# A fused adaLN + block-sparse FFN kernel: x loads one slot closer to their use, and the logits of the early batches turned and ranked behind the layer

## What is computed

```
z1 = einsum('bfi,bir->bfr', x, v) / 512
z  = einsum('bfr,bor->bfo', z1, u) / 16
y  = gelu(einsum('bfi,oi->bfo', x, W) + fc_bias + z + b)      # the layer
prob = softmax(y @ w_router + b_router); idx = top_k(prob, 4)  # the router
h = relu(einsum('nd,ebd->neb', y, w1b) + b1b)
out = x + einsum('neb,ebd,ne->nd', h, w2b, mask(idx)) + b2
```

## Time and profile before

| | us |
|---|---|
| three runs | 1649.1, 1648.52, 1642.79 (median 1648.52) |
| the profiled execution, its own time | 1648.12 |
| span of the profile | 1646.3 |
| PE busy | 951.5 (58%) |
| DVE busy | 837.2 (51%) |
| ACT / POOL busy | 583.9 / 576.1 (35% each) |
| granted TensorE clock, mean | 0.785 |
| DMA queues of SP / POOL, share of 16 engines | 38.5% / 21.2% |

### The profile page before, as it was taken

How to read it: one execution, slowest core, us unless ns; L and a number is a source line. 1 busy time by engine, 2 the same in 40 slices (tenths; PEclk the granted TensorE clock), 3 DMA queues, 4 the chain that set the end, 5 groups by cost and what they waited for, 6 DMA issues and landing times.

```text
span 1646.3 us, 17908 instructions
## 1 busy us (share of the span) xinstructions
PE 951.5 (58%) x4924; PEld 765.4 (46%) x4924; DVE 837.2 (51%) x1966; ACT 583.9 (35%) x1063; POOL 576.1 (35%) x589
## 2 busy tenths in 40 slices
PE   8755656466556465565565479866888898400000
PEld 7543545355445354454354357654777777300000
DVE  4432333333334242343343346563786786698777
ACT  6332333233233242333333245552665566200000
POOL 0554431332333323243423426556444344400000
PEclk9977787787777777787777789987999999755555
DMA  5765443534543534434434557657668765799999
GB/s 188 257 236 188 147 162 121 177 126 147 170 143 143 170 107 166 162 135 159 167 120 153 176 185 249 237 210 257 223 223 271 263 209 204 273 419 427 425 430 395
DMA packets 103234, 354.82 MB, mean 216 GB/s; under 512 B 29961, under 2 KB 29961, under 8 KB 92384
## 3 DMA queue, kind: packets, MB, share of 16 engines
q1 hardware_dynamic: 59104, 217.21, 38.5%
q0 software_dynamic: 43936, 136.37, 21.2%
q10 hardware_dynamic: 96, 0.10, 0.0%
HBM read 200.47 MB, written 169.65 MB: 225 GB/s over the span
## 4 chain that ended last, share of the span: by engine, by line
PE 39%; DMA 26%; issue 11%; DVE 8%; another core or an unknown queue 6%; SPq 5%; ACT 4%; POOL 1%; ACTq 1%; DVEq 0%; POOLq 0%
DMA tabi<-table 15%; PE hid L1310 9%; PE trn L1294 8%; PE lay L1204 8%; DMA w2l<-yt 8%; PE yps L1341 5%; PE hid L1315 3%; DVE xs L813 2%; PE hid L1190 1%; DVE stx L1026 1%; PE trn L1224 1%; ACT xs L585 1%; DMA outT<-ys 1%; PE lay L1341 1%
## 5 line engine op out<-in xcount | busy, mean ns | idle before, releaser
L547 POOL DMA_INDIRECT yt<-ys,ids x238 | 256.0, 1076 | 450.0 <-ACT ys L690 332.0
L1294 PE MATMUL trn<-idf,gr 128*128 128x128 f32 x720 | 127.8, 334 | 354.8 <-DMA tabi<-table 327.5
L521 POOL DMA_INDIRECT xg<-grow,ix x224 | 219.5, 980 | 231.5 <-DVE ix L909 167.5
L1294 PEld LDWEIGHTS trn<-idf,gr 128*128 128x128 f32 x720 | 105.5, 173 | 373.7 <-DMA tabi<-table 335.6
L1204 PE MATMUL lay<-w2l,xs 128*128 128x512 f32 x768 | 199.6, 411 | 0.0
L1204 PEld LDWEIGHTS lay<-w2l,xs 128*128 128x128 f32 x768 | 147.9, 198 | 31.0
L633 ACT ACTIVATE gsb<-trn 128x512 fp32r<-128x512 f32 x144 | 81.0, 598 | 190.8 <-PE trn L1294 187.5
L844 DVE TENSOR_TENSOR above<-gr,tabi 128x12 f32<-128x12 int32 x45 | 7.6, 169 | 263.5 <-DMA tabi<-table 263.5
L633 ACT ACTIVATE xs<-trn 128x512 fp32r<-128x512 f32 x88 | 50.4, 597 | 211.5 <-PE trn L1294 160.5
L835 DVE TENSOR_TENSOR gsb<-trn,gsb 128x512 fp32r<-128x512 f32 x144 | 94.5, 686 | 55.4 <-ACT gsb L633 48.9
L663 ACT ACTIVATE hv<-hid,b1c 128x512 f32<-128x512 f32 (+1 forms) x94 | 52.7, 584 | 191.2 <-PE hid L1315 159.8
(11 more groups left out here) (220 smaller groups left out, 2026.0 us busy)
## 6 DMA issues: line engine op xcount, KB each, us to landing
gr<-xg SPq DMA_DIRECT2D x45, 1056.0 KB
xs<-yt SPq DMA_DIRECT2D x16, 2048.0 KB, 19.8
w2l<-yt SPq DMA_DIRECT2D x15, 2048.0 KB, 20.2
grow<-xg SPq DMA_DIRECT2D x45, 528.0 KB
stx<-xT SPq DMA_DIRECT2D x64, 256.0 KB, 4.9
outT<-ys SPq DMA_DIRECT2D x31, 512.0 KB, 21.0
xg<-xrow SPq DMA_DIRECT2D x16, 528.0 KB
w2f<-xrow SPq DMA_DIRECT2D x16, 512.0 KB, 14.8
```

The lines of the kernel that those rows point to most:

```text
L521: pool.indirect_dma_start(out=xg, out_offset=bass.IndirectOffsetOnAxis(ap=ix[:, row_buffer(b), q, k:k + 1], axis=0), in_=grows[row_buffer( ...
L547: pool.indirect_dma_start(out=yt, out_offset=bass.IndirectOffsetOnAxis(ap=ids[:, j % 8, c:c + 1], axis=0), in_=yss[result_buffer(j)][:, c, ...
L1294: last = pe.transpose(trn[n % 2][:, k * P:(k + 1) * P], grs[j][:, c, k * P:(k + 1) * P], idf[:, :])
```

## The change

Six edits, and they fall in three groups. (1) **SP**: `load_x` moves behind `load_u`, `load_v` and the weight loads of its slot; in slots 0 to 26 it still loads x for slice s+6, slot 27 loads none, and from slot 28 on it loads slice s+5. (2) **Early batches**: in slots 0 to 26 PE's `turn_logits` moves from the end of slot q = 1 to behind the layer of q = 2, and `ranks` from the end of q = 2 to behind the layer of q = 3 (and in slot 27 behind its layer); the router of q = 3 moves behind `turn_batch`; ACT's `likelihoods` moves behind Gelu and `take_batch`; DVE's `choose`, `choose_rest` and `place` move to match, `place` by one slot. (3) **Tiles from 48 on**: PE's register loads of the expert's number move from the start of the slot, ahead of `turn_tile`, to behind `ffn1`.

```diff
@@ SP @@
             for s in range(LAG + NTILE):
-                if s + 6 < SLOTS:
-                    load_x(s + 6)
                 if q == 2 and b + 1 < NB:
                     load_u(b + 1)
...
                     sp.dma_start(w2f[:, s - 2, :], w2T[s - 2]).then_inc(s_ws, 16)
+                if s < LAG - 1:
+                    load_x(s + 6)
+                elif LAG <= s < SLOTS - 5:
+                    load_x(s + 5)
@@ ACT, slots 0 to 26 @@
-                if q == 2 and 1 <= b:
-                    likelihoods(b - 1)
                 gelu(s)
...
                     take_batch(s - 1)
+                if q == 2 and 1 <= b:
+                    likelihoods(b - 1)
@@ DVE, slots 0 to 26 @@
-                if q == 2 and 1 <= b:
-                    choose(b - 1)
                 split_x(s + 4)
...
-                if q == 2 and 1 <= b:
-                    choose_rest(b - 1)
-                if q == 3 and 1 <= b:
-                    full_tiles(b - 1)
...
                     logits(b - 1)
+                if q == 2 and 1 <= b:
+                    choose(b - 1)
+                    choose_rest(b - 1)
+                if q == 3 and 1 <= b:
+                    place(b - 1)
+                    full_tiles(b - 1)
                 if q == 3:
                     split_u(b + 1)
-                if q == 2 and 1 <= b:
-                    place(b - 1)
@@ DVE, slots 27 to 64 @@
-                if q == 3 and s >= LAG:
+                if q == 3:
                     place(b - 1)
@@ PE, turn_tile @@
                     pe.wait_ge(s_gr[j % 2], rows_in(j))
-                    if j >= PRE:
-                        expert[j] = []
-                        for h in range(experts(j)):
-                            pe.reg_load(r[2 * (j % 3) + h], tabi[0:1, j % 2, h, 0:1])
-                            expert[j].append(pe.snap(r[2 * (j % 3) + h], min_val=0, max_val=NE - 1))
...
+            def read_experts(j):
+
+                expert[j] = []
+                for h in range(experts(j)):
+                    pe.reg_load(r[2 * (j % 3) + h], tabi[0:1, j % 2, h, 0:1])
+                    expert[j].append(pe.snap(r[2 * (j % 3) + h], min_val=0, max_val=NE - 1))
@@ PE, slots 0 to 26 @@
-                if s % 2 == 1 and 3 <= s:
+                if q == 1 and 1 <= b:
                     router(s - 2)
+                if q == 2 and 1 <= b:
+                    turn_logits(b - 1)
+                if q == 3 and 1 <= b:
+                    ranks(b - 1)
                 if 1 <= s:
                     turn_batch(s - 1)
+                if q == 3:
+                    router(s - 2)
                 if q == 3 and 1 <= b:
                     counts(b - 1)
-                if q == 1 and 1 <= b:
-                    turn_logits(b - 1)
-                if q == 2 and 1 <= b:
-                    ranks(b - 1)
@@ PE, slot 27 @@
                     layer(s)
+                if s == LAG - 1:
+                    ranks(b - 1)
@@ PE, slots 65 to 100 @@
                     ffn1(j)
+                if PRE <= j + 1 < NTILE:
+                    read_experts(j + 1)
```

## The result

The change makes the kernel faster: 1378.5 us in the median of four runs (1370.0 to 1383.8) against 1645.7, a ratio of 0.837 with a 95% interval of 0.832 to 0.843. The forecast was 1339 us in a range of 1280 to 1430. The profiled execution took 1370.0 us with a span of 1368.2.

A forecast was written before the change was run, and what follows sets the result against it. No engine was full; in slots 27 to 57 PE waited for tile loads queued behind an x load waiting for DVE. 1646.3 - 312 + 3 + 4 - 4 = 1337 us span, plus 1.8: 1339 us, range 1280 to 1430.

The forecast's parts named there:

- Layer 27: Early batches, slots 7 to 27: moved logits and ranks keep the cycle's links, first cycle starts later; +4 us.
- Its rival, a cycle of 22 us set by POOL: Early batches: PE's late signals are avoided and the cycle falls to 22 us; 63 us less, 1275 us; chance 0.12.
- Slots 27 to 57: Tile load freed from the x load's wait: 31 slots at 14.6 us, 453 against 765 us, -312 us.
- Slots 59 to 62: Four slots of the kernel before without the suspected wait, 14.1 us each, used to price a dense slot; taken as unchanged.
- The first rival, dense slots worse than the four seen,: Slots 27 to 57 take 17 to 18.5 us, 97 us over the forecast, 1410 to 1460 us; chance 0.2.
- The sign I had named for it: Listed as showing the forecast wrong: "remote" waits on ACT and DVE of more than 4 us a slot.
- The lower bound of a slot: Dense slots not under 12.6 us, PE's own work; 62 us less than forecast over 31 slots.
- Edit 3: Register loads moved behind `ffn1`, 23 tiles with two each: between 0 and 9 us saved, half taken, -4 us.
- Slot 58: It now has an x load ahead as well: 14.6 us instead of 11.1, +3 us.
- The rule on TensorE's clock that the forecast weighed: Clock halves on an idling engine and returns when busy; dense slots would be nearer 13 us; forecast stayed at 14.6.
- The rule that spoke for the first rival: Completion lands after earlier writes of its DMA engine, so scatters in flight would hold back the tile load's signal.
- The rival that ended slower, late signals on every slot,: PE's signals 12 us late in each dense slot: 26.2 us a slot, +47 us, 1695 us; chance 0.03.

The follow-up runs named there:

- Edit 1 alone: The kernel before with only SP's new order of x loads: 1182.8 us, ratio 0.770, in a job without late signals.
- its opposite: The changed kernel with SP's old order, so the early-batch and register-load changes alone: 1539.5 us, ratio 1.003.
- two other ways to the same freedom: Changed kernel, x load at the slot's head, new distance: 1178.2 us; kernel before, x load of slice s+6 behind the tile's load: 1179.2 us; both ratio 0.767.
- the first job: Runs made together for the main result, with late signals: kernel before 1645.7 us, changed kernel 1378.5 us, ratio 0.837.
- the kernel with the tile's load in front: Kernel before with SP and register-load changes, no early-batch change, tile's load first in its slot: 1159.5 us (0.757); with late signals 1345.0 us (0.817).
- the cut layer: Layer without its third product: kernel before 1615.4 us (0.986); SP and register-load changes with tile's load first 1334.6 (0.813) and 1348.7 us (0.818).

## Why the prediction was right, and where it was off

The direction and the mechanism held: an x load that waits for the end of DVE's slot, in front of the tile's load in one queue. Edit 1 alone, its opposite, and two other ways to the same freedom all agree. The number held for jobs with late signals, on whose trace it was built: its ratio, 0.812, lies between the 0.837 of the first job and the 0.773 of a job without them, and 1186 us would have lain outside the range. Against the profiled execution the forecast of the span was 31 us low (1337 for 1368.2), and the terms account for it:

- **Layer 27**: forecast +4, measured +3.8 (215.1 to 218.9). The closeness is in part luck, since the parts came out otherwise. The cycle of the early batches kept its links. POOL's first scatters of three batches, changed kernel:

```profile
114.17 0.95 POOL L523 DMA_INDIRECT xg<-ys,ix  x1 [12.73 <-DVE ix L911]
146.15 0.96 POOL L523 DMA_INDIRECT xg<-grow,ix  x1 [10.32 <-DVE ix L911]
181.50 0.96 POOL L523 DMA_INDIRECT xg<-grow,ix  x1 [14.16 <-DVE ix L911]
```

  They are 32.0 and 35.4 us apart; 34.2 before. Over four cycles the mean is 33.4 us (33.2 before), so the cycle hardly grew, where the forecast had 0.6 us for each. The first one began 5.4 us later and not 3.4: POOL waited 42.1 us for its first scatter and 36.8 in the kernel before. Ahead of layer 27 stands PE's wait for tile 0, which the forecast had not counted, and `ranks` of the last batch is now behind it:

```profile
214.80 1.97 PE L1289 MATMUL trn<-idf,gr 128*128 128x128 f32 x8 [20.07 <-DMA tabi<-table]
```

  It was 4.05 us before, and the first scatter behind `ranks` comes 15.7 us later than before (225.26 for 209.59). Where no signals are late the sign holds too: layer 27 at 161.0 us with edit 2 and 152.3 without, in one job, 8.7 us later, of which 6.2 are left at layer 28. Edit 2 costs a little and gives nothing. Its rival, a cycle of 22 us set by POOL, came true in the job without late signals, but for both kernels: POOL scattered without a pause from 43.8 to 165.3 us in the kernel before, with the table's scatters 22.1 us apart.
- **Slots 27 to 57**: forecast 31 x 14.6 = 453 us, measured 473.4. This is the term that was mis-sized. Thirty slots took 15.04 us, and I had 14.6: 13 us. Late signals explain it in kind: in the job without them the same slots took 12.9 us. The 0.5 us added for the x and u loads was near: in that kind of job slots 28 to 57 take 0.7 to 1.0 us more than slots 59 to 62, in five kernels. The first slot, from layer 27 to layer 28, took 22.0 us (22.7 before) and not 14.6, 7.4 us more: I had let the gain begin one slot too early. Before, PE waited 8.41 us in it for tile 1. That wait is gone, but PE then waits 0.67 and 2.75 us for DVE and 3.19 us ahead of L1190 for nothing that the profile names, and L1190 itself takes 3.63 us instead of 2.10, so nearly nothing is left of the gain. The last two of PE's waits in that slot:

```profile
227.11 0.95 PE L1224 MATMUL trn<-idf,grow 128*128 128x128 f32 x4 [2.75 <-DVE gsb L837]
237.51 3.63 PE L1190 MATMUL hid<-xs,w2l 128*96 128x512 f32 x8 [3.19 <-issue]
```

- **Slots 59 to 62** were taken as unchanged and took 63.4 us instead of 56.6, 7 us more. It is not shown that the change did this. The four slots took 57.2 to 60.9 us in the other four traces with late signals (three of them with the cut layer), among them 58.5 behind long slots, and 47.9 to 48.0 us behind either kind of slot where no signals were late. The four slots that I used as the measure of a dense slot, 14.1 us, were the best of their kind.
- **The first rival, dense slots worse than the four seen,** came in a small form: its place was right (late signals, ACT's and DVE's "remote" waits), its size, 0.4 us a slot, far less than the 2.4 to 3.9 I had given it. The sign I had named for it, more than 4 us of such waits a slot, was nearly reached, with 106.7 us in 30 slots, 3.6 each. It was a poor sign: slots 59 to 62 of the kernel before have 20.9 us of such waits, 5.2 each, and are shorter.
- **The lower bound of a slot**, 12.6 us of PE's own work, was no bound: in the job without late signals slots 59 to 62 take 12.0 us and the kernel with the tile's load in front 12.4. PE's busy time had been read at a granted clock of 0.97, with late signals.
- **Edit 3**: forecast -4. From layer 63 to the end the three kernels without it, in jobs without late signals, took 559.8 to 561.5 us, and the five with it 550.7 to 555.6: in the mean 7.5 us less, within the bounds of 0 and -9. In the first job nothing of it is to be seen, 598.4 and 599.1, nor in the whole time of edit 1 with and without it (ratio 0.770 both, in two jobs without late signals).
- **Slot 58**: forecast 14.6, measured 13.4.

The rest, 8.5 us between the profiled execution and the median of the four runs, is the spread of the runs.

The rule on TensorE's clock that the forecast weighed (the Trainium skill, "TensorE: Matmul & The Clock Gate", Part 1) is borne out: the clock rose with the idle time gone, 0.76 to 0.93. The 13 us a slot that it pointed to were reached only where no signals were late, 12.9 us at 0.98. The rule that spoke for the first rival (the Trainium skill, "DMA: Bandwidth & Descriptors", "Queues, rings and completion order": a completion lands after every earlier write of its DMA engine) cost little: with the DMA share up from 0.44 to 0.70 PE waited 8.5 us in all for tiles. Whether completions were held back behind other waits no run here shows.

The rival that ended slower, late signals on every slot, did not come: it needed 10.4 us a slot, and the difference between the two kinds of job is 15.04 - 12.90 = 2.1 us.

## What to carry to other kernels

In a hand-ordered program, look at each in-order DMA queue for a load that waits for the end of a stage, and at what stands behind it: the cost falls on the latter, and the trace shows it as a wait for a transfer of ordinary length. Put the load with the nearest use first, or shorten the prefetch distance of the other by one; both gave 23% in a job without late signals. If a slot somewhere in the trace lacks the suspected wait, it prices the change, but four slots of one trace are a small sample: here the same four took 56.6 to 63.4 us in different traces of one kind. And before two times are compared, compare the kernel before in both jobs.

## What the runs showed of the hardware

The same program took 1534 to 1536 us in two jobs and 1637 to 1646 in three. What differs most in the traces is when PE's finished signals arrive. In the jobs with late signals ACT and DVE wait up to 15.3 us for an unnamed sender, in clusters beside runs of POOL's scatters. For `fu` (L863, L865) the sender can only be PE, since the instruction waits for PE's signals alone: it starts 12.7 us behind the recorded end of the router's matmuls in the batch of the earlier trace rows, and 14.0 us behind it in the changed kernel's worst case (a matmul's end is modelled by the profile). Gelu can also wait for a scatter from its row buffer, so not every "remote" wait need be PE's. The one of the earlier trace rows ended 2.6 us behind the last scatter. The changed kernel's longest such waits ahead of slot 27 were these:

```profile
DVE fu L865 <- remote: 41.2, 5, 15.3
DVE lmax L870 <- remote: 26.6, 3, 11.0
```

In the jobs without late signals POOL scatters without a pause too, from 43.8 to 165.3 us in the kernel before, and nothing is late, so the scatters are not enough to cause it. In the kernel before, slots 28 to 57 have no such wait in the first job either. The x loads landed later as well: in the median 4.9 and 4.3 us behind their issue in the first job (kernel before, changed kernel), 2.8 and 3.6 in the job without late signals. What causes it stays open. It was in none of the kernels' edits, and no run here separated it. The number of the chip does not decide it: chip 2 had a job of 1536 us and the one of 1637. Between the two kinds the kernel with less slack, the changed one, differs by more, 192 us against 112.
